# Trace back: GpSimd makes the table of exits in four pieces while VectorE makes the maps

## What is computed

```python
D = _pairwise_euclidean(small, large)        # 256 x 256 per sequence
R = _dtw_cost(D)                             # r = d + min(up, left, diag), row by row
i_idx, j_idx, valid = _backtrack(R, T_small, T_large)   # from the last cell back to the first
contrib = small[i_idx] * valid[:, None]
expanded = zeros.at[j_idx].add(contrib)
```

## Time and profile before

| | us |
|---|---|
| median of 3 runs | 1656.24 (1652.63 to 1657.77) |
| the profiled execution | 1667.43 |
| its span | 1665.7 |
| DVE busy | 1000.0 (60%) |
| PE busy | 1109.3 (67%) |
| POOL busy | 665.6 (40%) |

### The profile page before, as it was taken

One profiled execution on the slowest core, in us unless ns is written; L12 is line 12 of the kernel. 1 busy time (PEld: TensorE's weight loads), 2 busy tenths in 40 slices (PEclk: granted clock), 3 DMA queues, 4 the chain that ended last, 5 costly groups with the idle time before them and its releaser, 6 DMA issues. The chain is left out here.

```text
span 1665.7 us, 23182 instructions
## 1 busy us (share of the span) xinstructions
PE 1109.3 (67%) x5635; PEld 816.2 (49%) x5636; DVE 1000.0 (60%) x2044; ACT 584.9 (35%) x1336; POOL 665.6 (40%) x719
## 2 busy tenths in 40 slices
PE   3657776777776617740168158898888888888970
PEld 1223332333332416630157057787877787777870
DVE  2999999899989408889686862222222232222326
ACT  3757767677666414410145001111111111111110
POOL 5877775876866100000130143332333233333330
PEclk9899999999999755555596589998999899989995
DMA  5533555445645111211322005665467446656518
GB/s 173 183 120 127 151 163 158 135 148 140 175 140 149 48 31 26 45 32 37 128 88 102 0 7 181 223 207 184 155 227 255 156 163 240 210 191 224 192 42 302
DMA packets 168161, 235.57 MB, mean 141 GB/s; under 512 B 30320, under 2 KB 95920, under 8 KB 167568
## 3 DMA queue, kind: packets, MB, share of 16 engines
q1 hardware_dynamic: 152056, 205.82, 39.4%
q0 software_dynamic: 8784, 24.00, 4.1%
q10 hardware_dynamic: 7240, 4.71, 0.9%
HBM read 205.24 MB, written 25.03 MB: 138 GB/s over the span
## 5 line engine op out<-in xcount | busy, mean ns | idle before, releaser
L1784 PE MATMUL mo_h<-mo_xt,w 128*128 128x128 f32 x2912 | 370.0, 282 | 15.3 <-issue 13.9
L1784 PEld LDWEIGHTS mo_h<-mo_xt,w 128*128 128x128 f32 x2912 | 358.3, 197 | 40.6 <-issue 30.3
L839 PE MATMUL st_y_ps<-st_hc,ident 128*128 128x512 f32 x512 | 269.5, 653 | 147.7 <-DVE st_hc L460 147.7
L452 DVE TENSOR_TENSOR_SCAN st_h<-st_da,st_u 128x512 f32<-128x512 f32 x256 | 297.8, 1204 | 41.7 <-POOL st_u L348 32.2
L348 POOL TENSOR_TENSOR st_u<-st_dx,codes 128x1024 f32<-128x1024 f32 x128 | 298.4, 2357 | 56.9 <-DMA codes<-bc 34.2
L1822 ACT ACTIVATE mo_silu<-mo_h 128x128 f32<-128x128 f32 x364 | 101.1, 278 | 526.2 <-PE mo_h L1784 515.2
L1844 DVE TENSOR_TENSOR mo_inter<-mo_silu,mo_h 128x128 f32<-128x128 f32 x364 | 102.9, 287 | 264.0 <-ACT mo_silu L1822 242.5
L839 PEld LDWEIGHTS st_y_ps<-st_hc,ident 128*128 128x128 f32 x512 | 93.0, 199 | 283.5 <-DVE st_hc L460 211.6
L1792 PE MATMUL mo_o_ps<-wo,mo_inter 128*128 128x256 f32 x728 | 206.6, 387 | 5.3 <-DVE mo_inter L1844 5.1
L585 ACT ACTIVATE st_da<-st_delta,st_a_neg 128x510 f32<-128x510 f32 x256 | 171.9, 685 | 81.0 <-DVE st_h L452 76.0
L460 DVE TENSOR_TENSOR st_hc<-st_h,st_cps 128x1024 f32<-128x1024 f32 x128 | 152.7, 1193 | 0.1
(11 more groups left out here) (246 smaller groups left out, 1287.9 us busy)
## 6 DMA issues: line engine op xcount, KB each, us to landing
codes<-bc SPq DMA_DIRECT2D x256, 256.0 KB, 4.6
w<-in_L_ffn_w_dram SPq DMA_DIRECT2D x128, 512.0 KB
wo<-in_L_ffn_wo_dram SPq DMA_DIRECT2D x64, 512.0 KB
co_got<-outs SPq DMA_DIRECT2D x16, 512.0 KB, 9.1
x<-in_x_dram SPq DMA_DIRECT2D x8, 512.0 KB, 8.9
st_cx<-in_ctx_dram SPq DMA_DIRECT2D x8, 512.0 KB, 4.9
dist<-st_dd SPq DMA_DIRECT2D x8, 512.0 KB, 3.3
codes<-wv_code SPq DMA_DIRECT2D x32, 128.0 KB, 3.4
```

Source lines behind the costliest of these rows:

```text
L452: nc.vector.tensor_tensor_scan(h_sb[k % HRING][:, dh, :], da_ps[dh][:, :], u_sb[k % URING][:, dh, :], 0.0, ALU.mult, ALU.add).then_inc(h_o ...
L839: m = nc.tensor.matmul(y_ps[:, dh, :], K.ident[:, :], hc_sb[k % RING][:, dh, :], start=False, stop=(n == N - 1))
L1784: ins = nc.tensor.matmul(h_ps[m][:, i * P:(i + 1) * P], K.w[r][i][:, c_, m * P:(m + 1) * P], xt[:, c_, :], start=(c_ == 0), stop=(c_ == DC ...
```

## The change

The table of exits moves from DVE to POOL. POOL makes the product in four pieces of 8 rows (2048 elements per partition), waits for the first step of DVE (`up`), and then makes the sum in four pieces. DVE goes from the last map right to the entry chain, and waits for the four sums (`exits_ok`) only ahead of the walk. SP now waits for the four products (`codes_free` at 4) and for the last map (`mapped`), since both read `codes`.

```diff
         @block.sync
-            sp.wait_ge(codes_free, 1)
+            sp.wait_ge(codes_free, QS)
+            sp.wait_ge(mapped, 1)
...
         @block.gpsimd
...
+            by_row = lambda a, rows: K.codes[:, :, rows, a, :].rearrange("p s i j -> p i s j")
+            view = lambda x, rows: x[:, rows, :].rearrange("p i (s j) -> p i s j", j=SW)
+            pool.wait_ge(set_up, 6)
+            for k in range(QS):
+                rows = slice(k * BR // QS, (k + 1) * BR // QS)
+                nc.gpsimd.tensor_tensor(view(exits, rows), by_row(0, rows),
+                                        col_dg[:, :].rearrange("p (a s j) -> p a s j", a=1, j=SW).broadcast_to(
+                                            [P, BR // QS, SEG, SW]), ALU.mult).then_inc(codes_free, 1)
+            pool.wait_ge(st, 1)
+            for k in range(QS):
+                rows = slice(k * BR // QS, (k + 1) * BR // QS)
+                pool.wait_ge(codes_free, k + 1)
+                nc.gpsimd.tensor_tensor(exits[:, rows, :], exits[:, rows, :], up[:, rows, :],
+                                        ALU.add).then_inc(exits_ok, 1)
...
         @block.vector
...
-            did(nc.vector.tensor_tensor(view(exits), by_row(0),
-                                        col_dg[:, :].rearrange("p (a s j) -> p a s j", a=1, j=SW).broadcast_to(
-                                            [P, BR, SEG, SW]), ALU.mult))
-            dve.wait_ge(st, n[0])
-            dve.sem_inc(codes_free, 1)
-            did(nc.vector.tensor_tensor(exits[:, :, :], exits[:, :, :], up[:, :, :], ALU.add))
-
+            dve.wait_ge(st, n[0])
+            dve.sem_inc(mapped, 1)
             did(nc.vector.tensor_copy(entry[:, :], K.entry0[:, :]))
...
+            dve.wait_ge(exits_ok, QS)
             for i in reversed(range(BR)):
```

More of the change, by code:

```diff
@@ L1120, in trace_back @@
         codes_free = sem("tb_codes_free")
+        exits_ok, mapped = sem("tb_exits_ok"), sem("tb_mapped")
+        QS = 4
         gathered = sem("tb_gathered")
```

## The result

The changed kernel takes 1675.9 us (median of 4 runs, 1673.5 to 1679.4); the kernel before 1654.4 (4 runs, 1650.7 to 1657.8). The ratio is 1.0132, with a 95% interval of 1.0099 to 1.0165: **slower by 21.5 us**, where 25.9 were forecast, inside the stated range.

What follows compares the result with a forecast made beforehand. DVE's instruction list was taken to bound trace back, parted from its neighbours by barriers. -8.9 (exits removed) + 36.2 (POOL's pieces) - 1.4 (hidden) = +25.9 us on 1656.24 gave 1682.1 us, range 1671 to 1695.

Steps and rivals of the forecast that it cites:

- The stage is DVE's list, and the exits cost 8.9 us on it: Trace back lasts as long as DVE's instructions; removing the two on the exits gives -8.9 us.
- POOL and DVE don't run side by side where both read SBUF: In trace back, shared SBUF ports let only one engine move, so all eight POOL pieces, 36.2 us, fall on the path.
- Eight instructions of 4 to 5 us, the rest untouched: Profile sign in DVE's maps: eight or so of 97 instructions lengthen, others stay; maps grow from 40 to about 75 us.
- 36.2 us for eight pieces: POOL's exits in trace back: 4.53 us per 2048-element piece, from 32-bit rows at 2.12 ns an element; +36.2 us.
- the stated lower bound (29.1): POOL's exits at 1.69 ns an element, from a memset's pace: 3.6 us a piece, 29.1 us for eight.
- 1.4 us hidden at the changes of turn: Where POOL and DVE alternate in the maps, 0.18 us of each of eight pieces overlaps; -1.4 us.
- The load of the context is hidden: SP's load, now starting after the last map, takes 16.2 us under 34.5 us of later DVE work; costs nothing.
- no contention: Rival: POOL works beside the maps at no cost, leaving only -8.9 us, 1647.4 us; chance 6%.
- DVE keeps the turn: Rival: POOL can't get in between DVE's maps and works after them, delaying the walk; +21.4 us, 1677.6 us; chance 14%.
- scans don't contend: Rival: each POOL piece hides one DVE scan of 0.69 us in the maps; +20.7 us, 1676.9 us; chance 9%.
- A slower POOL in 16 bits: Rival: POOL's exit pieces take up to 5.8 us each in 16 bits; +36.2 us, 1692.4 us; chance 10%.

Runs made afterwards that it cites:

- Experiment 9: Kernel before, with the exits made by TensorE matmuls and ScalarE instead of DVE; stage 79.1 us, whole 1624.1 us, ratio 0.9800 to the kernel before.
- 5: Kernel before plus 16 POOL memsets into a spare tile beside the maps, reading nothing; stage 87.7 us, whole 1655.6 us (1 run), before 1654.0.
- 7: Changed kernel with maps and first candidates in 32-bit PSUM, exits still on POOL; stage 87.8 us, whole 1656.5 us, ratio 1.0004 to the kernel before.
- experiment 1: Changed kernel, but DVE waits for all eight POOL pieces before starting the maps; stage 110.9 us, whole 1676.7 us, ratio 1.0096 to the kernel before.
- experiment 2: Changed kernel with POOL's product and sum as one 8192-element instruction each, not four; stage 109.7 us, whole 1676.1 us, ratio 1.0101 to the kernel before.
- experiment 6: Kernel before plus eight POOL copies of 2048 16-bit elements in SBUF beside trace back; stage 100.2 us, whole 1681.8 us (1 run), before 1654.0.

## Why the prediction was right

The forecast of 1682.1 us set out from 1656.24, 1.8 us over the median given above; the rest of the distance to 1675.9 is the change itself, +21.5 where +25.9 were forecast.

- *The stage is DVE's list, and the exits cost 8.9 us on it*: right. Experiment 9 takes them away from DVE and the stage gains 8.6.
- *POOL and DVE don't run side by side where both read SBUF*: right, and shown from both sides, by taking the reads from POOL (5: no stall) and from DVE (7: no stall), and by running them one after the other (1: 1.8 us more, no more). That the stall is the whole of POOL's instruction is shown by experiment 2.
- *Eight instructions of 4 to 5 us, the rest untouched*: right, 3.94 to 4.42. The maps grew to 70 us, where 75 were named.
- *36.2 us for eight pieces*: too high by 4.2 us, and this term is the miss of 4.4 us but for two small ones that follow. The 32-bit slope of 2.12 ns an element was carried over to 16 bits; measured are 1.90 ns, 4.03 us a piece and 32 for eight, which the stated lower bound (29.1) allowed for.
- *1.4 us hidden at the changes of turn*: 1.9 measured (in experiment 1 DVE stands idle for 31.9 us while POOL works alone; 30.0 lie on the path here). The removed 8.9 came with about 0.2 us of new gap ahead of the entry chain. The sum by measured terms is -8.9 + 31.9 - 1.9 + 0.2 = 21.3 us, and the stage grew by 21.4.
- *The load of the context is hidden*: right. It now starts at 801.15, and the barrier comes as soon after the walk as before (4.46 us).
- *The rivals*: no contention is out. That DVE keeps the turn is out: POOL got in after each single DVE instruction. In time this rival was nearer than the forecast (+21.4 where +21.5 came out), though wrong in mechanism, and only the timeline tells them apart. That scans don't contend is out: they stood for 4.40 and 4.42 us. A slower POOL in 16 bits is out: it is a little faster.

## What to carry to other kernels

Before work moves from VectorE to an idle GpSimd, look at what the two read. Where VectorE's instructions beside it have two operands in SBUF (or are a `tensor_scalar` like that of the earlier trace rows, which has one and stood all the same, 2.80 us and not 0.68) and GpSimd's read SBUF at all, the move adds GpSimd's full time to VectorE's path, and neither the order nor smaller pieces helped here. What helps is to take one side's reads away from SBUF, or to take engines beside which VectorE's durations stay as they are: here TensorE and ScalarE made the same table at no cost to the stage. The stall shows as busy time, so compare the shortest and the longest duration of one and the same instruction.

## What the runs showed beyond that

- How the two engines take turns depends on whether GpSimd's next instruction is ready. In the changed kernel a piece's wait has been met when the piece before it ends, and every VectorE instruction stood until they were done. Where GpSimd first had to wait for its own last instruction (the copies of experiment 6, and the sum after the product in experiment 2), one VectorE instruction of 0.28 us slipped through: after every second stall there, and once here.
- TensorE's matmuls of 512 columns with 16-bit operands show durations of 0.60 to 0.63 us, at a granted clock of 0.5, which is the lower level, 1.2 GHz. The durations overlap: 48 of them filled 24 us, 0.50 us each.
- Work that serves nothing can change another stage: 48 matmuls with their activations, in a stage in which TensorE is idle, made the kernel 1.35% faster, with 20 packets on the instruction queue and not 47. So an experiment that adds instructions has to be read stage by stage.
